# Turning x with TensorE, two tiles in every body, into a second transposed copy

## The reference

```python
qkv = (x @ w_qkv).reshape(b, n, 3, H, hd).transpose(2, 0, 3, 1, 4)
attn = jnp.einsum('bhnd,bhmd->bhnm', q, k) * scale
attn = jnp.where(attn_mask[None, None] == 0, -jnp.inf, attn)
attn = jax.nn.softmax(attn, axis=-1)
o = jnp.einsum('bhnm,bhmd->bhnd', attn, v).transpose(0, 2, 1, 3).reshape(b, n, d)
o = o @ w_proj + b_proj
ln = (o - mu) * jax.lax.rsqrt(var + LN_EPS) * ln_gamma + ln_beta
return o + ln            # and around it: layernorm(x + ref(x))
```

## Time and profile before

| | before |
|---|---|
| median of 3 runs | 3227.46 us |
| profiled execution, its own time | 3231.68 us |
| its span (first to last instruction) | 3229.8 us |
| granted TensorE clock, mean | 0.973 |
| busy: PE, DVE, ACT, POOL | 93%, 68%, 81%, 81% |
| DMA transposes of `p_split`, of `x_split` | 1024, 64 |

### The profile page before, as it was taken

One profiled execution on the slowest core, in us unless ns is written; L12 is line 12 of the kernel. 1 busy time (PEld: TensorE's weight loads), 2 busy tenths in 40 slices (PEclk: granted clock), 3 DMA queues, 4 the chain that ended last, 5 costly groups with the idle time before them and its releaser, 6 DMA issues.

```text
span 3229.8 us, 119607 instructions
## 1 busy us (share of the span) xinstructions
PE 2994.3 (93%) x42112; PEld 1842.0 (57%) x42112; DVE 2197.0 (68%) x4243; ACT 2624.1 (81%) x3790; POOL 2628.1 (81%) x1610
## 2 busy tenths in 40 slices
PE   5889999899998999999999998999999899999995
PEld 2556556565565556656566565556556566565562
DVE  4546667677676767767677676767767677676775
ACT  5878878788787878878788787888888788787882
POOL 4768878788787878878798797888878788787884
PEclk9989999999999999999999999999999999999997
DMA  8999999999999999999999999999999999999994
GB/s 225 192 199 195 211 214 218 218 208 220 211 212 218 215 214 219 216 212 219 214 216 214 215 213 222 216 215 220 216 214 219 212 212 219 212 215 218 216 208 108
DMA packets 2320778, 682.49 MB, mean 211 GB/s; under 512 B 2268498, under 2 KB 2268498, under 8 KB 2320724
## 3 DMA queue, kind: packets, MB, share of 16 engines
q1 hardware_dynamic: 2266724, 581.58, 97.3%
q10 hardware_dynamic: 54000, 100.16, 9.7%
HBM read 77.60 MB, written 33.55 MB: 34 GB/s over the span
## 4 chain that ended last, share of the span: by engine, by line
POOL 54%; issue 29%; SPq 7%; PE 6%; DMA 2%; DVE 1%; POOLq 1%; ACT 1%; ACTq 0%; DVEq 0%
POOL p_split L742 42%; SPq L307 5%; POOL x_res L758 4%; POOL x_split L776 4%; POOL norm L766 2%; POOL norm L761 2%; PE scores_a L401 1%; PE side L360 1%; SPq L285 1%; DMA pt<-p_split 1%; PE side L347 1%; POOL shift L769 1%; POOLq L741 1%; PE proj L383 0%; PE pv_bank L422 0%
## 5 line engine op out<-in xcount | busy, mean ns | idle before, releaser
L742 POOL TENSOR_TENSOR p_split<-p,p_split 128x1024 f16<-128x1024 f32 x1024 | 2172.4, 2138 | 531.8 <-ACT p_split L507 526.0
L494 ACT ACTIVATE p<-p,row_min 128x1024 f32<-128x1024 f32 x1024 | 1167.9, 1142 | 91.9 <-DVE row_min L638 89.8
L507 ACT ACTIVATE p_split<-p 128x1024 f16<-128x1024 f32 x1024 | 1053.6, 1046 | 206.8 <-DMA pt<-p_split 205.9
L638 DVE CUSTOM_DVE_ANT_0 p<-scores_a,mask_q 128x1024 f32<-128x1024 f32 x512 | 626.9, 1224 | 502.3 <-PE scores_b L401 481.9
L422 PE MATMUL pv_bank<-v_both,pt 128*128 128x64 f16 x8192 | 840.0, 195 | 26.5 <-DMA pt<-p_split 24.6
L424 PE MATMUL pv_bank<-v_both,pt 128*128 128x64 f16 x8192 | 840.6, 195 | 0.0
L423 PE MATMUL pv_bank<-v_both,pt 128*128 128x64 f16 x8192 | 840.5, 195 | 0.0
L422 PEld LDWEIGHTS pv_bank<-v_both,pt 128*128 128x128 f16 x8192 | 747.9, 99 | 115.2 <-issue 39.6
L360 PE MATMUL side<-xt,w_hi 128*128 128x512 f16 x2048 | 683.2, 391 | 119.3 <-DMA xt<-x_split 114.3
L423 PEld LDWEIGHTS pv_bank<-v_both,pt 128*128 128x128 f16 x8192 | 736.9, 99 | 84.4 <-issue 6.0
L424 PEld LDWEIGHTS pv_bank<-v_both,pt 128*128 128x128 f16 x8192 | 737.4, 99 | 0.0
(11 more groups left out here) (80 smaller groups left out, 4261.3 us busy)
## 6 DMA issues: line engine op xcount, KB each, us to landing
x_in<-in_x ACTq DMA_DIRECT2D x63, 512.0 KB, 5.1
x_res<-in_x ACTq DMA_DIRECT2D x120, 256.0 KB, 3.3
out<-x_res ACTq DMA_DIRECT2D x120, 256.0 KB, 3.7
pt<-p_split SPq DMA_TRANSPOSE x1024, 4.8
pt<-in_adj SPq DMA_DIRECT2D x8, 512.0 KB, 9.7
ot<-in_L_gnn_w_qkv SPq DMA_DIRECT2D x4, 768.0 KB, 9.8
p<-in_x SPq DMA_DIRECT2D x4, 512.0 KB, 5.3
p<-in_x ACTq DMA_DIRECT2D x8, 256.0 KB, 8.5
```

The lines of the kernel that those rows point to most:

```text
L494: nc.scalar.activation(p32[:, slot, :], p32[:, slot, :], ACT.Exp, bias=row_min[:, slot:slot + 1], scale=-1.0, accum_out=row_sum[:, head:he ...
L507: nc.scalar.activation(p_split[:, head % RING, HI, :], p32[:, head % RING, :], ACT.Copy).then_inc(hi_done, 1)
L638: nc.vector.tensor_tensor_reduce(out=p32[:, slot, :], in0=scores[ab][:, :], in1=mask_q[:, u, :], scale=-SCALE, scalar=3.0e38, op0=ALU.add, ...
L742: nc.gpsimd.tensor_tensor(p_split[:, slot, LO, :], p32[:, slot, :], p_split[:, slot, HI, :], ALU.subtract).then_inc(lo_done, 1)
```

## The change

`x_split` is gone. `xt` has a second copy in its room (a dimension for the parity of the batch). In each body of batches 0 to 14 TensorE turns the two float32 tiles of `x_in` itself (X0, X1: four transposes each), through the `side` banks; ScalarE writes the high part from PSUM into the other copy of `xt`, VectorE the low part. So there are ten kinds in `side` instead of eight, ScalarE has two takes of 128x512 instead of one pass over 128x1024, VectorE two more operations, and GpSimd's split is gone. SyncE has no DMA transposes of x, and its conditional is gone. Q0 waits for X1 in every body. `ORDER`, `COST` and the take slots are adjusted, and the hardware loop is bodies 5 to 58 (four bodies fewer). In the start, TensorE turns the eight first tiles, and VectorE's work on the weights is mixed with their low parts.

```diff
-ORDER = [("Q1", 0, 12), ("V0", 0, 48), ("V1", 0, 48), ("P0", 0, 4), ("O1", 0, 4), ("P0", 4, 13), ("Q0", 0, 12),
-         ("K0", 0, 12), ("K1", 0, 12), ("P1", 0, 9), ("O0", 0, 4), ("P1", 9, 13)]
+ORDER = [("Q1", 0, 12), ("X0", 0, 4), ("V0", 0, 48), ("V1", 0, 48), ("P0", 0, 4), ("O1", 0, 4), ("P0", 4, 9),
+         ("X1", 0, 4), ("P0", 9, 13), ("Q0", 0, 12), ("K0", 0, 12), ("K1", 0, 12), ("P1", 0, 9), ("O0", 0, 4),
+         ("P1", 9, 13)]
-LOOP = (PAIRS + 1, GROUPS - 1)
+LOOP = (PAIRS + 1, GROUPS - PAIRS - 1)
-TAKE_ACT = {"Q1": 5, "V0": 10, "V1": 10, "O1": 13, "Q0": 19, "K0": 29, "K1": 29, "O0": 30}
-TAKE_DVE = {"Q1": 6, "V0": 10, "V1": 12, "O1": 14, "Q0": 22, "K0": 29, "K1": 29, "O0": 30}
-SPLIT_ACT, SPLIT_POOL = 8, 10
-XT_UNIT = [3, 3, 4, 4]
+TAKE_ACT = {"Q1": 3, "X0": 7, "V0": 10, "V1": 10, "O1": 14, "X1": 15, "Q0": 20, "K0": 28, "K1": 29, "O0": 30}
+TAKE_DVE = {"Q1": 4, "X0": 7, "V0": 10, "V1": 11, "O1": 14, "X1": 15, "Q0": 22, "K0": 29, "K1": 30, "O0": 30}
+LOAD_X = 18
-        x_split = sb("x_split", [P, T // 2, 2, 2, D], F16)
-        xt = sb("xt", [P, T, 2, KC, P], F16)
+        xt = sb("xt", [P, 2, T, 2, KC, P], F16)
...
-            for p in range(T // 2):
-                turn_x(FIRST_GROUP, p)
...
+            def first_turn(t):
+                pe.wait_ge(x_first_loaded[t], 16)
+                wait(pe, x_first_lo, t - 1)
+                for k in range(KC):
+                    mm = nc.tensor.transpose(side[t % 2][:, k * P:(k + 1) * P], x_first[:, t, k * P:(k + 1) * P], ident[:, :])
+                mm.then_inc(x_first_turned, 1)
...
+                elif kind[0] == "X":
+                    if i == 0 and half == 0:
+                        wait_alone(pe, x_in_loaded, g * 16 + 16)
+                    mm = nc.tensor.transpose(bank[:, i * P:(i + 1) * P], x_in[:, half, i * P:(i + 1) * P], ident[:, :])
...
-                    mm = nc.tensor.matmul(bank[:, c * P:(c + 1) * P], xt[:, t, rows, k, :], w[:, k, OF_V, pair(g), :],
+                    mm = nc.tensor.matmul(bank[:, c * P:(c + 1) * P], xt[:, parity(batch(g)), t, rows, k, :],
+                                          w[:, k, OF_V, pair(g), :],
...
-                    if i == 0 and kind == NEXT_FIRST:
-                        wait_alone(pe, x_turned[0], batch(g + 1) * 32 + 32)
-                    if i == 0 and kind == "K1":
-                        wait_alone(pe, x_turned[1], batch(g + 1) * 32 + 32)
+                    if i == 0 and kind == NEXT_FIRST and active(g, "X1"):
+                        wait_alone(pe, side_dve, side_done(g, "X1"))
...
-                                          xt[:, 4 * half:4 * half + 4, x_half, k, :],
+                                          xt[:, parity(batch(of)), 4 * half:4 * half + 4, x_half, k, :],
...
+                elif kind[0] == "X":
+                    nc.scalar.activation(xt[:, parity(batch(g + PAIRS)), pair(g) * 2 + half, HI, :, :],
+                                         bank[:, :].rearrange("p (k n) -> p k n", k=KC), ACT.Copy).then_inc(side_act, 1)
...
+                elif kind[0] == "X":
+                    at, tile = parity(batch(g + PAIRS)), pair(g) * 2 + half
+                    nc.vector.tensor_tensor(xt[:, at, tile, LO, :, :], bank[:, :].rearrange("p (k n) -> p k n", k=KC),
+                                            xt[:, at, tile, HI, :, :], ALU.subtract).then_inc(side_dve, 1)
```

More of the change, by code:

```diff
@@ L233, in bodies @@
                 body(g)
[L235 to L241, removed]
         def heads(g, u, ab):
@@ L272, in _ @@
         def _(sp):
-            for t in range(T // 2):
-                sp.dma_start(x_first[:, t, :, :], x_pairs[t, :, :, :]).then_inc(x_first_loaded[t], 16)
+            for t in range(T):
+                sp.dma_start(x_first[:, t, :], x_tiles[t, :, :]).then_inc(x_first_loaded[t], 16)
             for kc in range(KC):
@@ L312, in body @@
                 for u in range(UNITS):
-                    for p in range(T // 2):
-                        if u == XT_UNIT[p] and not (known(g) and g == FIRST_GROUP):
-                            transposing(sp, g, lambda: turn_x(g, p))
                     ug, uk = unit_before(g, u, 1)
@@ L425, in times_v @@
                 mm.then_inc(pv_done, 1)
+            for t in range(T):
+                first_turn(t)
             def body(g):
@@ L454, in prepare_projection, with first_high @@
                                      scale=WSCALE).then_inc(bias_ready, 1)
[L456 to L465 removed]
+            def first_high(t):
+                act.wait_ge(x_first_turned, t + 1)
+                nc.scalar.activation(xt[:, 0, t, HI, :, :], side[t % 2][:, :].rearrange("p (k n) -> p k n", k=KC), ACT.Copy
+                                     ).then_inc(x_first_hi, 1)
             def take(g, kind):
@@ L715, in body @@
                     if known(g) and g == FIRST_GROUP and s == 0:
-                        prepare_weights()
+                        for t in range(T):
+                            first_low(t)
+                            if t % 2:
+                                prepare_weights(t // 2)
                         for t in range(T):
@@ L770, in layer_norm @@
                                             ).then_inc(shifted, 1)
-            def split(g):
-                if known(g) and not 0 <= batch(g) < B - 1:
-                    return
-                wait_alone(pool, x_hi_done, g + PAIRS + 1)
-                nc.gpsimd.tensor_tensor(x_split[:, pair(g), :, LO, :], x_in[:, :, :], x_split[:, pair(g), :, HI, :],
-                                        ALU.subtract).then_inc(x_lo_done, 1)
-            for p in range(T // 2):
-                pool.wait_ge(x_hi_done, p + 1)
-                nc.gpsimd.tensor_tensor(x_split[:, p, :, LO, :], x_first[:, p, :, :], x_split[:, p, :, HI, :],
-                                        ALU.subtract).then_inc(x_lo_done, 1)
             def body(g):
```

75 lines of the change are left out of this document (31 added, 44 removed).

## The result

| | before | after |
|---|---|---|
| median of 10 runs each | 3231.32 us | 3246.96 us |
| ratio, 95% interval | | 1.005 (1.004 to 1.0061) |
| profiled span | 3229.8 us | 3246.3 us |
| most ordinary loop bodies / the turn body | 46.06 / 55 to 58 | 49.20 / 49.20 |

The forecast was 3200 us, faster, with a range of 3165 to 3244. The kernel became 0.5% slower. The page after: busy time, SyncE's queue of transposes, and the first line of the chain of waits.

What follows compares the result with a forecast made beforehand. PE was taken to bound the ordinary body, with 46.2 us of matmuls. Terms -145 + 55 + 81 - 13 - 5 = -27 gave 3205 us for the profiled execution, 3200 against the median; range 3165 to 3244 us.

Steps and rivals of the forecast that it cites:

- The transposes of x by DMA go: In 15 turn bodies the wait, the slow clock behind it and the crowded queue go: -145 us.
- TensorE turns x: Eight float32 transposes in each of 60 bodies, 0.115 us each on the bound engine: +55 us.
- Where O0 waits: Ahead of O0, one more matmul of P1 shortens PE's idling for K0's low part: -13 us (0 to -50).
- The start: At the kernel's start, the mask's second half is issued and finished 4.5 us earlier: -5 us (0 to -8).
- Registers in front of PE's matmuls: Register instructions for xt in V, Q and K cost 1.5 us in 54 loop bodies: +81 us (0 to +200).
- The takes: ScalarE's and VectorE's reads of side banks: no engine becomes the bound; hand-overs finish tenths of a us early, priced with registers.
- the two small estimates: Register losses per loop body: 0.7 to 1.5 us over V's stretch and 0.4 us at Q0.
- the prediction's own border: Loss per loop body from which the starved rival, not the forecast (0.9 to 2.3 us), holds: 2.3 us.
- PE starved by its own sequencer: Rival, chance 0.20: late side-bank waits remove the lead at V and Q0; 2.8 us a body gives 3270 us.
- The lead hides the registers: Rival, chance 0.24: the sequencer's lead covers the register instructions; loop body 46.9 us, time 3124 us.
- Another chain paces the body: Rival, chance 0.08: scores, exponential, low part, transposes need 48 us a body and hide registers; 3190 to 3225 us.
- the signs named for the register term: Loop bodies 47.8 to 49.2 us, unrolled 59 to 62 some 46.9, issue-ended holes at V and Q0, 56 fused operations.

Runs made afterwards that it cites:

- the last version: Against the kernel after: V mixed with long matmuls, no Q0 wait for X1, VectorE's X0 take later, P0's last matmul ahead of X1; 3145.03 us, 0.9732 of before.

## Why the prediction was wrong

- *The transposes of x by DMA go*, -145: right, 152 measured alone.
- *TensorE turns x*, +55: right. 480 transposes of 0.116 us are 56.
- *Where O0 waits*, -13: right. The hole fell by one matmul of P1, from 0.45 to 0.23 us.
- *The start*, -5: right. The mask is complete at 34.3 instead of 38.0 us, the first row extreme 3.9 us earlier.
- *Registers in front of PE's matmuls*, +81: this step failed. The span grew by 16.5; with the four terms above (-152 + 56 - 13 - 4) there remain 130 us, 2.4 for each of the 54 loop bodies where 1.5 were taken. The other count, 49.20 less 46.76 (46.06 + 0.92 - 0.22), gives the same 2.4. That the unrolled bodies pay nothing was not right either: 60 to 62 are some 2 us longer than loop bodies of the kernel before, which is 6 of the 130 us.

In its own parts: V lost 1.8 us (11.4 against 9.6) where 0.7 to 1.5 were put, and Q0 0.50 to 0.57 where 0.4 was put.

The registers themselves had the right size: 1.54 us added to the kernel before, 1.58 taken from the one after, 1.37 of it in V. What was missing is the step before it. In *The takes* the prediction says of the hand-overs that each is done some tenths of a us before PE wants it, and that it prices this with the next term; there it only took the two small estimates. But "before PE wants it" is too late. What must be let go in time is the sequencer, and from the end of the take to Q0's first matmul, with five register instructions in between, it needs 0.65 to 0.68 us (1239.27 to 1239.95; 2016.34 to 2016.99). For Q0's wait a run shows it: without the wait the body is 0.32 us shorter. For V0's opening, where 0.53 us stay without xt's registers, it is read from the trace: Q1's low part ends at 2005.81, and no run takes that wait away. These two, and 0.13 us within P0, are the 0.86 us that stayed. A late take and the registers behind it are not two cases but one sum. By the prediction's own border (2.3 us a body) it is the rival *PE starved by its own sequencer*, at its lower end, that came true. It was given 0.20, among other things because "the groups of products between let the sequencer catch up". They do, but only for the next twelve matmuls of V, and they do nothing for V0's opening, which stands before the first of them.

*The lead hides the registers* is refuted: its body was 46.9 us, and 49.20 came. By the Trainium skill, "TensorE: Matmul & The Clock Gate", Part 1, TensorE's queue holds 64 instructions. No run here shows its depth, but the lead it would give was not there, as V's registers cost 1.37 us. *Another chain paces the body* is refuted as well: the same takes and transposes run in bodies of 47.4 us in the last version, and the long hole at Q0 ends by issue. Of the signs named for the register term, the loop body (49.2), its holes and the 56 fused operations appeared; of the unrolled bodies only 59 did (46.6). The waits for Q1 and X1 did not show as VectorE's, since they end before the array is idle.

What stays open: the last version's loop body is still 1.0 us above its unrolled body 59 (0.21 in front of Q0, 0.10 within X0, some 0.45 in V); how much the wait for Q1 costs V0 by itself; and whether it is code fetching that slows long code.

## What to carry to other kernels

When an address in a hardware loop becomes dynamic, count the register instructions in front of the short matmuls, and look at what stands just ahead: long matmuls pay for them, a group of short products pays for few, and a wait that is taken late for none. A wait is late for the sequencer well before it is late for the array, so place it, and drop it where other waits imply it, by the sequencer's time plus the registers behind it. Read distances between starts, and compare a loop body with an unrolled one: a busy share of 96% hid 2.4 us in every 49.

## What the hardware showed that was not expected

- Eight bodies in one loop iteration made the kernel after 2% slower and the kernel before 8%: a hole such as that of 3.7 us where the next iteration begins, 360 packets of instructions instead of 60, and SyncE's issue of a transpose at a mean of 2.83 us in unrolled bodies 59 to 62 against 2.58 in the loop.
- Eight more float32 transposes in a body of 47.6 us cost 0.11 us, since they stood where the sequencer was behind.
- Moving Q0 and O0 by one matmul each cost 48 us (3246.96 to 3294.79): a group of products of 0.7 us and one long matmul had hidden a hand-over.
